# One fused layer on one core: projection weights in one transfer, the head in token halves, a new order of VectorE's attention steps

## The chip, the core and the metric
The kernel runs on one core of a Trainium2 chip. A core has five instruction streams: TensorE (PE; its weight loads are listed as PEld), VectorE (DVE), ScalarE (ACT), GpSimd (POOL) and SyncE (SP). They work side by side and wait for one another only through semaphores. The metric is the device time of one execution in microseconds (us), lower is better.

## The reference, cut to what matters
Input x is 2 sequences of 512 tokens with 256 channels, fp32. "norm" is a layer norm without weights.

```
x = x + attn(norm(x))                    # attn(y) = softmax(causal q k^T / 16) v @ o_proj + y
                                         #   q, k, v = (norm(y) * gamma + beta) @ qkv
x = x + ffn(norm(x))                     # ffn(y) = fp8w(down)((silu(y @ fp8w(gate) * s) * (y @ fp8w(up) * s))) * s
x = x + conv(norm(x))                    # conv(y) = y convolved along 512 steps with a kernel made of
                                         #   exp(dt * A), A from a_real_log, a_imag; C from c_re, c_im; + D * y
x = x + ffn(norm(x))
```

fp8w is a rounding of the weights to the fp8 grid. The convolution's time axis is the one of length 2, so only two taps of its kernel matter.

## The kernel before, in words
Tokens lie in 8 tiles of 128 rows, tiles 0 to 3 for the first sequence, 4 to 7 for the second. Every engine has its program written out by hand; the order of the calls in it is the order of the work, and there is no planner.

**Loads.** SP issues them in this order (lines 231 to 256): tiles 0-1 of x, the q part of `qkv`, tiles 2-3, the k part, four small parameter rows, the v part, tiles 4-7, `o_proj`, scale rows, the gate, up and down weights (768 KB each) and the down scales. ACT issues three small ones (L523 to L527). POOL issues c_re and c_im in `constants` (L287).

**Head.** PE first runs transposes of the identity (`warm_up`, L1065; 14, and 8 more between the q and the k part). `turn_w` (L1073) transposes one part of the projection weights, `fold` (L1080) multiplies q's by k's (`wqk`) and v's by `o_proj` (`wvo`). Tiles are normalised (statistics on DVE, L710 and L713; the inverse deviation by `inverse_std` on POOL, L296 to L306; the scaling by DVE L718 or ACT L539), transposed (`turn_z`, L1088), copied with gamma and beta to `xn_cols` (ACT L510, DVE L729), and multiplied by `wqk` (`make_g`, L1097) and `wvo` (`make_v`, L1104). Each product is copied out of PSUM in two pieces, one by ACT and one by DVE (`g_part`/`g_chunk`, `v_part`/`v_half`).

**Attention loop.** For tile k PE makes `scores` (L1139, with the causal mask L1141), DVE takes the row maxima (`row_max`, L868), ACT the exponentials (`exp_scores`, L577), PE transposes them (`turn_probs`, L1152), ACT copies them (`copy_probs`, L585), PE multiplies by v (`attend`, L1164), DVE finishes the tile (`attention_out`, L873, L876 and its statistics), POOL gives `inverse_std(1, ...)`, ACT normalises (`h_rows`, L569), PE transposes (`turn_h`, L1186), ACT copies the result (`copy_h`, L590) and DVE makes the remainder (`h_tails`, L863).

**Beside it.** DVE computes the parameters of the convolution (`exp_reduce`, `exp_finish`, `exp_times_dt`, `reduce_angle`), the fp8 grids of the three weight matrices (`grid_begin`, `grid_end`, L790 and L795) and lifts and lowers the down weights onto theirs in two halves (`lift_down`, L803; `lower_down`, L809, the last of which is the signal `down_rounded` 2). POOL rounds gate and up (`round_weight`, L413 and L416), makes `x_plus_scales` (L400 to L404), and then in one sequence: `inverse_std(1, 0, 2)`, `taps_begin`, a power (L441), `inverse_std(1, 2, 2)`, a wait for `fit_ready` (DVE's `fit_powers`) and for `down_rounded` 2, six multiplications `down16` (L446), `inverse_std(1, 4, 2)`, `taps_middle`, `inverse_std(1, 6, 2)`, `taps_end` (last line L384) and the first `tail` of the ffn (L456).

**FFN passes.** Four passes of four tiles (two ffn layers). A pass multiplies by gate and up (L1224, 24 blocks of 128 columns in six steps m) and by down (L1258, three steps behind). In pass 0, `spread_taps` (L1269) stands on PE behind step m = 4 of gate and up and waits for the taps; the `down` behind it needs POOL's first tail, which stands behind `taps_end` in POOL's program:

```
if n == 0 and m == 4:
    spread_taps()          # waits for taps_ready
if m >= LAG:
    down(n, m - LAG)       # m - LAG = 1 here: POOL's tail
```

The first gate product with `h_head` waits for both `copy_h`, its product with `h_tail` for both `h_tails`.

Of the kernel before, what the change touches and what calls it, by code (L numbers as in the profile page):

```python
# [34 lines left out]
WARM_UP = 14  # L35
WARM_BETWEEN = 8
# [9 lines left out]
def hybrid_layer(nc, x, qkv, o_proj, gamma, beta, d_param, log_dt, a_real_log, a_imag, c_re, c_im,  # L46
# [13 lines left out]
    with ctx:  # L60
# [48 lines left out]
        param_rows = sb("param_rows", [4 * C, P])  # L109
        params = sb("params", [P, 4 * C])  # L110
        gammas, betas, log_dts, d_params = (params[:, C * n:C * n + C] for n in range(4))
# [33 lines left out]
        q_loaded, k_loaded, v_loaded, wo_loaded = sem("q_loaded"), sem("k_loaded"), sem("v_loaded"), sem("wo_loaded")  # L145
# [19 lines left out]
        w_turned_pe, w_turned_ready = sem("w_turned_pe"), sem("w_turned_ready")  # L165
# [29 lines left out]
        BANK_WT, BANK_WQK, BANK_WVO, BANK_PARAMS, BANK_SCALES, BANK_NORMS = [4, 5, 3], 2, 3, 7, 4, 5  # L195
        BANK_Z = [[0, 1], [4, 5]]
        BANK_G = [[6, 7], [0, 1]]
# [31 lines left out]
        def _(sp):  # L229
# [14 lines left out]
            load_chunks(qkv_sb[:, :, 0:KEY], qkv[:, 0:KEY], q_loaded)  # L244
            load_x(1)
            load_chunks(qkv_sb[:, :, KEY:2 * KEY], qkv[:, KEY:2 * KEY], k_loaded)
            load_rows(param_rows, (gamma, beta, log_dt, d_param), params_loaded)
            load_chunks(qkv_sb[:, :, 2 * KEY:], qkv[:, 2 * KEY:], v_loaded)
            load_x(2)
            load_x(3)  # L250
            load_chunks(wo_sb[:], o_proj, wo_loaded)
# [3 lines left out]
            load_chunks(down_raw[:], down_w, w_loaded[2])  # L255
            sp.dma_start(down_scale_all[:], down_scale.partition_broadcast(P)).then_inc(down_scale_loaded, 16)
# [16 lines left out]
        def _(pool):  # L273
# [11 lines left out]

            def load_s4d(n, array, loaded):
                pool.dma_start(s4d_in[:, n, :].rearrange("p (c n) -> p c n", c=C),  # L287
                               array.rearrange("(c p) n -> p c n", p=P)).then_inc(loaded, 16)
# [97 lines left out]
            def constants():  # L386

                load_s4d(2, c_re, c_loaded)
                load_s4d(3, c_im, c_loaded)
# [43 lines left out]
            inverse_std(0, T, T, twice=True, negative_mean=True)  # L433
            round_weight(0, gate16, gate_up_ready)
            x_plus_scales()
# [3 lines left out]
            taps_begin()  # L439
            pool.wait_ge(bound_squared, 1)  # L440
            pool.tensor_tensor(bound[:, 4, :], bound[:, 3, :], pos_half[:], ALU.pow).then_inc(bound_ready, 1)  # L441
            inverse_std(1, 2, 2, negative_mean=True)
# [58 lines left out]
        def _(act):  # L501
            def turned(w):
                act.wait_ge(w_turned_pe, w + 1)
                act.activation(w_turned[:, w, :, :].rearrange("p c n -> p (c n)"), psum[:, BANK_WT[w], :],
                               ACT.Copy).then_inc(w_turned_ready, 1)

            def xn_chunk(b):
                act.wait_ge(params_ready, 1)
                act.wait_ge(z_turned, C * b + 1)
                act.activation(xn_cols[:, b, 0, :], psum[:, BANK_Z[b][0], :], ACT.Identity, scale=gammas[:, 0:1],  # L510
                               bias=betas[:, 0:1]).then_inc(xn_by_act, 1)

            def g_part(b):
                act.wait_ge(g_made, C * b + 1)
                act.activation(g_cols[:, b, 0, :], psum[:, BANK_G[b][0], :], ACT.Copy,
                               scale=float(KEY) ** -0.5).then_inc(g_by_act, 1)
# [5 lines left out]

            act.dma_start(e_in[:, 0:HN].rearrange("p (c n) -> p c n", c=C),  # L523
# [6 lines left out]
            turned(1)  # L530
            act.wait_ge(tanh_in, 1)
            act.activation(s4d[:, 3, :], s4d[:, 2, :], ACT.Tanh, scale=0.5).then_inc(tanh_out, 1)
            act.wait_ge(wqk_made, 1)
            act.activation(wqk[:].rearrange("p c n -> p (c n)"), psum[:, BANK_WQK, :], ACT.Copy).then_inc(wqk_ready, 1)
            xn_chunk(0)
            turned(2)
# [4 lines left out]
            act.wait_ge(wvo_made, 1)  # L541
            act.activation(wvo[:].rearrange("p c n -> p (c n)"), psum[:, BANK_WVO, :], ACT.Copy).then_inc(wvo_ready, 1)
            g_part(0)
            xn_chunk(1)
# [5 lines left out]
            v_part(0)  # L550
            act.wait_ge(scales_turned, 1)
            act.activation(scales[:], psum[:, BANK_SCALES, 0:2 * M], ACT.Copy).then_inc(scales_ready, 1)
# [40 lines left out]
            square_weights(0)  # L593
            exp_scores(0)
            g_part(1)
            square_weights(1)
            exp_scores(1)
# [4 lines left out]
            for k in range(2, K):  # L602
                exp_scores(k)
                copy_probs(k - 1)
# [87 lines left out]
        def _(dve):  # L692
# [33 lines left out]
            def xn_chunk(b):  # L726
                dve.wait_ge(params_ready, 1)
                dve.wait_ge(z_turned, C * b + 2)
                dve.tensor_scalar(xn_cols[:, b, 1, :], psum[:, BANK_Z[b][1], :], gammas[:, 1:2], betas[:, 1:2],  # L729
                                  ALU.mult, ALU.add).then_inc(xn_by_dve, 1)  # L730

            def g_chunk(b):
                dve.wait_ge(g_made, C * b + 2)
                dve.tensor_scalar(g_cols[:, b, 1, :], psum[:, BANK_G[b][1], :], float(KEY) ** -0.5, None,
# [147 lines left out]
            normalise((0, 1))  # L882
            first_stats(2)
            exp_reduce()
            normalise((2, 3))
            dve.wait_ge(params_turned, 1)
            dve.tensor_copy(params[:], psum[:, BANK_PARAMS, 0:4 * C]).then_inc(params_ready, 1)
# [22 lines left out]
            for k in range(2, K):  # L910
# [4 lines left out]
                if k == K - 1:  # L915
                    fit_powers()
# [417 lines left out]
```

## Time and profile before

| | |
|---|---|
| median of 3 runs | 127.04 us (126.94 to 127.36) |
| the profiled execution | 126.93 us |
| its span in the trace | 125.1 us |
| projection weights' first transposes on PE | 4.79 us |
| first gate product of pass 0 | 51.95 us |
| `spread_taps` | 61.51 us |

The span runs from the first to the last instruction of the core; the 1.8 us by which the execution's time is longer lie around it. All times of rows are counted from the span's start.

### The profile page before, as it was taken

The page shows a single profiled execution, that of the slowest core. Times are in us where ns is not written, and L with a number is a line of the kernel's source. Part 1 is how long each engine was busy: PE and PEld are TensorE (multiplying, and loading weights), DVE is VectorE, ACT ScalarE, POOL GpSimd, SP SyncE. Part 2 cuts the span into 40 slices and gives each one's busy share as a digit, 9 for nine tenths or more (in the row PEclk, how much of TensorE's full clock was granted, in tenths as well). Part 3 has the DMA queues.
Part 4 walks back from the last instruction along what each step waited for, and adds up shares of the span by engine and source line. Part 5 has one row for each costly group of instructions (what it writes and reads, how often), then busy time and mean ns, then how long its engine had stood idle before and what let it go on. Part 6 is the DMA issues. An engine that isn't in the chain of part 4 may idle for free. (4 is left out here: it accounts for less than half of the span.)

```text
span 125.1 us, 2125 instructions
## 1 busy us (share of the span) xinstructions
PE 116.7 (93%) x682; PEld 77.8 (62%) x682; DVE 96.8 (77%) x228; ACT 77.6 (62%) x147; POOL 85.1 (68%) x166
## 2 busy tenths in 40 slices
PE   5996999999999999999999999979999899999970
PEld 5874458668568768645769545567445479755540
DVE  0499999919765876949798889998889965783792
ACT  2325089694874469858865279873587773659800
POOL 2246569999999889888433779697985780037931
PEclk9999999999999999999999999999999999999999
DMA  3999920000000000000000000000000000000404
GB/s 86 305 330 340 339 80 8 0 0 0 0 0 0 5 0 5 0 0 0 0 0 5 0 0 0 0 3 5 0 0 0 3 0 5 0 0 0 168 0 168
DMA packets 5682, 5.80 MB, mean 46 GB/s; under 512 B 1140, under 2 KB 5160, under 8 KB 5672
## 3 DMA queue, kind: packets, MB, share of 16 engines
q1 hardware_dynamic: 4648, 5.52, 13.3%
q10 hardware_dynamic: 960, 0.15, 0.7%
q8 instruction: 5, 0.08, 0.3%
q0 software_dynamic: 64, 0.02, 0.1%
q14 instruction: 5, 0.04, 0.1%
HBM read 4.63 MB, written 1.05 MB: 45 GB/s over the span
## 5 line engine op out<-in xcount | busy, mean ns | idle before, releaser
L618 ACT ACTIVATE gated<-psum,scales 128x512 f32<-128x512 f32 x24 | 16.3, 680 | 12.4 <-PE psum L1224 10.1
L1258 PE MATMUL psum<-down,f_head 128*128 128x256 bf16 x96 | 22.2, 273 | 0.6 <-POOL f_tail L456 0.5
L1258 PE MATMUL psum<-down,f_tail 128*128 128x256 bf16 x96 | 22.1, 272 | 0.0
L456 POOL TENSOR_TENSOR f_tail<-fused,f_head 128x512 f16<-128x512 f32 x11 | 13.0, 1181 | 12.4 <-ACT f_head L624 10.7
L981 DVE SCALAR_TENSOR_TENSOR fused<-psum,up_scales_fit,gated 128x512 f32<-128x512 f32 (+1 forms) x25 | 17.7, 715 | 2.6 <-PE psum L1224 1.3
L624 ACT ACTIVATE f_head<-fused 128x512 f16<-128x512 f32 (+1 forms) x25 | 15.1, 607 | 2.0 <-DVE fused L981 1.7
L989 DVE TENSOR_TENSOR f_tail<-fused,f_head 128x512 f16<-128x512 f32 (+1 forms) x14 | 10.3, 741 | 5.8 <-ACT f_head L624 5.8
L1224 PE MATMUL psum<-h_head,up 128*128 128x512 f16 x44 | 13.1, 379 | 0.1
L1224 PE MATMUL psum<-h_tail,gate 128*128 128x512 f16 x44 | 13.1, 379 | 0.0
L1224 PE MATMUL psum<-h_head,gate 128*128 128x512 f16 x44 | 13.1, 379 | 0.0
L1224 PE MATMUL psum<-h_tail,up 128*128 128x512 f16 x44 | 13.1, 379 | 0.0
L301 POOL TENSOR_TENSOR rstd<-var_eps,neg_half 128x2 f32<-128x2 f32 (+1 forms) x15 | 11.2, 744 | 2.2
L1258 PEld LDWEIGHTS psum<-down,f_head 128*128 128x128 f16 x96 | 9.4, 98 | 4.6 <-POOL f_tail L456 2.1
L1164 PE MATMUL psum<-v_rows,probs_cols 128*128 128x256 f32 x40 | 10.3, 389 | 0.2 <-ACT probs_cols L585 0.2
L1258 PEld LDWEIGHTS psum<-down,f_tail 128*128 128x128 f16 x96 | 9.4, 98 | 1.7
L1139 PE MATMUL psum<-xn_cols,g_cols 128*128 128x128 f32 (+3 forms) x32 | 10.0, 436 | 0.0
L296 POOL TENSOR_SCALAR var_eps<-mean_var 128x2 f32<-128x2 f32 (+1 forms) x15 | 3.8, 256 | 8.7 <-DVE mean_var L713 7.8
L1164 PEld LDWEIGHTS psum<-v_rows,probs_cols 128*128 128x128 f32 x40 | 7.0, 190 | 2.3 <-ACT probs_cols L585 0.8
L1097 PE MATMUL psum<-xn_cols,wqk 128*128 128x512 f32 x16 | 7.4, 603 | 1.0 <-DVE xn_cols L729 1.0
L462 POOL TENSOR_TENSOR x<-scaled_down,x 128x256 f32<-128x256 f32 x8 | 5.6, 725 | 3.6 <-DVE scaled_down L933 3.6
L1224 PEld LDWEIGHTS psum<-h_head,up 128*128 128x128 f16 x44 | 4.2, 98 | 5.5 <-DVE fused L981 0.6
L1224 PEld LDWEIGHTS psum<-h_tail,gate 128*128 128x128 f16 x44 | 4.2, 98 | 5.3 <-DVE h_tail L863 0.4
(176 smaller groups left out, 266.0 us busy)
## 6 DMA issues: line engine op xcount, KB each, us to landing
x_in<-in_x SPq DMA_DIRECT2D x4, 256.0 KB, 4.2
qkv_sb<-in_qkv SPq DMA_DIRECT2D x3, 256.0 KB, 4.1
gate_raw<-in_gate_w SPq DMA_DIRECT2D x1, 768.0 KB, 7.1
up_raw<-in_up_w SPq DMA_DIRECT2D x1, 768.0 KB, 8.9
down_raw<-in_down_w SPq DMA_DIRECT2D x1, 768.0 KB, 10.6
out<-x_in SPq DMA_DIRECT2D x3, 256.0 KB, 2.1
wo_sb<-in_o_proj SPq DMA_DIRECT2D x1, 256.0 KB, 4.7
down_scale_all<-in_down_scale SPq DMA_DIRECT2D x1, 128.0 KB, 10.4
```

Source lines behind the costliest of these rows:

```text
L301: power = pool.tensor_tensor(rstd[:, n, k:k + count], var_eps[:, n, k:k + count], neg_half[:, 0:count], ALU.pow)
L456: pool.tensor_tensor(f_tail[:, m, :], fused[:, m % FUSED, :], f_head[:, m, :], ALU.subtract).then_inc(f_tail_by_pool, 1)
L462: pool.tensor_tensor(new[:, k, :], scaled_down[:, k, :], old[:, k, :], ALU.add).then_inc(ready, 1)
L618: act.activation(gated[:, m % 2, :], psum[:, BANK_GATE[m % 2], :], ACT.Silu, scale=gate_scales[:, m:m + 1]).then_inc(gated_ready, 1)
L624: act.activation(f_head[:, m, cols], fused[:, m % FUSED, cols], ACT.Copy).then_inc(f_head_ready, 1)
L981: dve.scalar_tensor_tensor(out=fused[:, m % FUSED, cols], in0=psum[:, BANK_UP[m % 2], cols], scalar=up_scales_fit[:, m:m + 1], in1=gated[: ...
L989: dve.tensor_tensor(f_tail[:, m, cols], fused[:, m % FUSED, cols], f_head[:, m, cols], ALU.subtract).then_inc(f_tail_by_dve, 1)
L1097: last = pe.matmul(column(BANK_G[b][j], 0, S), wqk[:, c, j * P:j * P + P], xn_cols[:, b, c, :], start=(c == 0), stop=(c == C - 1))
L1139: pe.matmul(column(BANK_S[k % 2], 0, W), g_cols[:, b, j, i * P:i * P + P], xn_cols[:, b, j, 0:W], start=(j == 0), stop=(j == C - 1))
L1164: last = pe.matmul(column(BANK_O[k % 2], 0, H), probs_cols[:, k % 2, t * P:t * P + P], v_rows[:, b, t, :], start=(t == 0), stop=(t == i))
L1224: last = pe.matmul(column(banks[m % 2], 0, S), w[:, c, m * P:m * P + P], part[:, c, :], start=(part is h_head and c == 0), stop=(part is h ...
L1258: last = pe.matmul(down_columns(n, t), part[:, m, t * P:t * P + P], down16[:, m, :], start=(m == 0 and (t % 2 == 0 or n == 2 * B - 1) and ...
```

## The change
The q, k and v parts come in one transfer behind tiles 0-1 of x, with tiles 2-3, `o_proj` and tiles 4-7 behind it. Gamma, beta and d_param rows are loaded by ACT ahead of its own three, the log_dt row is gone (it was not used), and c_re and c_im are loaded by SP behind the down weights. There are 17 warm-up transposes and none later. The first sequence's transposes, `xn_cols` and g are made in halves of two tiles, its v in two pieces, and tiles 0 and 1 are scored before the second half's g. k's turned weights are copied by DVE. DVE, ACT and POOL have new orders; PE has the `attend` of tile 6 ahead of the `turn_probs` of tile 7.

```diff
-WARM_UP = 14
-WARM_BETWEEN = 8
+WARM_UP = 17
...
-        BANK_WT, BANK_WQK, BANK_WVO, BANK_PARAMS, BANK_SCALES, BANK_NORMS = [4, 5, 3], 2, 3, 7, 4, 5
+        BANK_WT, BANK_WQK, BANK_WVO, BANK_PARAMS, BANK_SCALES, BANK_NORMS = [4, 5, 3], 2, 4, 7, 4, 5
-        BANK_G = [[6, 7], [0, 1]]
+        BANK_G = [[5, 2], [0, 1]]
...
             load_x(0)
-            load_chunks(qkv_sb[:, :, 0:KEY], qkv[:, 0:KEY], q_loaded)
+            load_chunks(qkv_sb[:], qkv, qkv_loaded)
             load_x(1)
-            load_chunks(qkv_sb[:, :, KEY:2 * KEY], qkv[:, KEY:2 * KEY], k_loaded)
-            load_rows(param_rows, (gamma, beta, log_dt, d_param), params_loaded)
-            load_chunks(qkv_sb[:, :, 2 * KEY:], qkv[:, 2 * KEY:], v_loaded)
+            load_chunks(wo_sb[:], o_proj, wo_loaded)
             load_x(2)
             load_x(3)
-            load_chunks(wo_sb[:], o_proj, wo_loaded)
...
             load_chunks(down_raw[:], down_w, w_loaded[2])
+            for n, array in ((2, c_re), (3, c_im)):
+                load_chunks(s4d_in[:, n, :].rearrange("p (c n) -> p c n", c=C), array, c_loaded)
...
@@ POOL
             inverse_std(0, T, T, twice=True, negative_mean=True)
+            x_plus_scales()
             round_weight(0, gate16, gate_up_ready)
-            x_plus_scales()
             angle_squares()
             round_weight(1, up16, gate_up_ready)
             inverse_std(1, 0, 2, negative_mean=True)
             taps_begin()
+            inverse_std(1, 2, 2, negative_mean=True)
             pool.wait_ge(bound_squared, 1)
             pool.tensor_tensor(bound[:, 4, :], bound[:, 3, :], pos_half[:], ALU.pow).then_inc(bound_ready, 1)
-            inverse_std(1, 2, 2, negative_mean=True)
             pool.wait_ge(fit_ready, 1)
             pool.wait_ge(down_rounded, 2)
...
@@ ACT
+            load_row(0, gamma)
+            load_row(1, beta)
+            load_row(2, d_param)
...
             turned(0)
-            turned(1)
+            turned(2)
+            xn_half(0)
+            (wqk, then wvo)
+            g_first_half()
             (tanh)
-            (wqk); xn_chunk(0); turned(2)
+            xn_half(1)
             (normed, tiles 4 to 7)
-            (wvo); g_part(0); xn_chunk(1)
+            v_part(0)
             (trig)
-            v_part(0); (scales)
+            xn_second()
             square_weights(0)
+            copy_scales()
             exp_scores(0)
-            g_part(1)
+            exp_scores(1)
+            g_part()
             square_weights(1)
-            exp_scores(1)
             copy_probs(0)
...
             for k in range(2, K):
-                exp_scores(k)
-                copy_probs(k - 1)
+                if k in (3, 6, 7):
+                    copy_probs(k - 1)
+                    exp_scores(k)
+                else:
+                    exp_scores(k)
+                    copy_probs(k - 1)
...
@@ DVE, the whole new order
             first_stats(0); normalise((0, 1)); copy_k(); copy_params(); xn_half(0)
             first_stats(2); first_stats(T); normalise((2, 3)); first_stats(T + 2)
             exp_reduce(); xn_half(1); exp_finish(); exp_times_dt(); reduce_angle()
             grid_begin(0); grid_end(0); row_max(0); row_max(1); g_second_half(); xn_second()
             grid_begin(1); v_half(0); grid_end(1); grid_begin(2); grid_end(2); g_chunk()
             row_max(2); attention_out(0); v_half(1); row_max(3); attention_out(1)
             row_max(4); lift_down(0); attention_out(2); magnitude()
             row_max(5); lift_down(1); attention_out(3); row_max(6); read_norms(); bound_gate_up()
             attention_out(4); row_max(7); lower_down(0); attention_out(5); fit_powers()
             h_tails(0, 0); lower_down(1); h_tails(0, 1); attention_out(6); attention_out(7)
...
@@ PE
-            turn_w(0, q_loaded)
-            warm_up(WARM_BETWEEN)
-            turn_w(1, k_loaded)
+            turn_w(0)
+            turn_w(1)
+            turn_w(2)
...
+            turn_z_half(0)
+            fold(wqk); fold(wvo)
+            make_g_half(0)
+            turn_z_half(1)
+            make_v(0, (0, 1))
...
+            scores(0)
+            scores(1)
+            pe.wait_ge(v_by_act, 1)
+            make_g_half(1)
+            turn_z()
+            make_v(0, (2, 3))
...
             make_g()
-            scores(1)
             turn_probs(0)
             make_v(1)
...
             turn_h(0, 0, first=True)
+            attend(K - 2)
             turn_probs(K - 1)
-            attend(K - 2)
             turn_h(0, 1, first=True)
             attend(K - 1)
```

Lines in brackets and the DVE and PE blocks stand for calls that the full diff writes out. `make_g_half(1)` waits for `v_by_act` because its PSUM bank (2) holds ACT's piece of v.

## Rows read from the trace of the kernel before

**Rows 1.** The page's first part: busy time of each engine over the span.
```profile
PE 116.7 (93%) x682; PEld 77.8 (62%) x682; DVE 96.8 (77%) x228; ACT 77.6 (62%) x147; POOL 85.1 (68%) x166
```

**Rows 2.** A windows table: each engine's busy time in one stretch of pass 0.
```profile
51.95:61.50 9.55, 9.55 (x49) 4.71 (x48) 7.10 (x12) 7.09 (x14) 7.72 (x29) 1.00 0.00 0
```

**Rows 3.** Timeline of PE in the head: start, duration, what, [idle before, releaser].
```profile
1.52 3.25 PE L1065 MATMUL psum<-ident 128*128 128x128 f32 x14 [1.52 <-POOL ident L282]
...
5.48 1.04 PE L1065 MATMUL psum<-ident 128*128 128x128 f32 x8
6.50 0.66 PE L1073 MATMUL psum<-ident,qkv_sb 128*128 128x128 f32 x4
...
10.13 0.60 PE L1073 MATMUL psum<-ident,qkv_sb 128*128 128x128 f32 x4
11.69 3.67 PE L1097 MATMUL psum<-xn_cols,wqk 128*128 128x512 f32 x8 [0.96 <-DVE xn_cols L729]
...
16.92 1.80 PE L1088 MATMUL psum<-ident,normed 128*128 128x128 f32 x8
18.77 3.72 PE L1104 MATMUL psum<-wvo,xn_cols 128*128 128x256 f32 x16
```

**Rows 4.** Timeline of PE in the attention loop and pass 0.
```profile
37.07 1.56 PE L1164 MATMUL psum<-v_rows,probs_cols 128*128 128x256 f32 x6 [0.23 <-ACT probs_cols L585]
...
50.22 1.89 PE L1164 MATMUL psum<-v_rows,probs_cols 128*128 128x256 f32 x8
51.95 0.59 PE L1224 MATMUL psum<-h_head,gate 128*128 128x512 f16 x2
...
61.51 1.05 PE L1269 MATMUL psum<-ident,taps 128*128 128x128 f32 x8
```

**Rows 5.** Timeline of POOL, from the head to pass 0.
```profile
13.50 0.21 POOL L296 TENSOR_SCALAR var_eps<-mean_var 128x4 f32<-128x4 f32 x1 [1.93 <-DVE mean_var L713]
...
17.14 5.16 POOL L413 TENSOR_TENSOR x<-gate_raw,grid 128x512 f32<-128x512 f32 x3 [1.01 <-DVE grid L795]
...
32.53 3.73 POOL L413 TENSOR_TENSOR scaled_down<-up_raw,grid 128x512 f32<-128x512 f32 x3
...
48.29 2.76 POOL L446 TENSOR_SCALAR down<-down_raw,bound 128x256 bf16<-128x256 f32 x6
...
56.05 0.73 POOL L298 TENSOR_SCALAR mean_rstd<-mean_var 128x2 f32<-128x2 f32 x1
...
59.69 0.19 POOL L384 TENSOR_SCALAR taps<-s4d 128x2 f32<-128x2 f32 x1
59.84 1.16 POOL L456 TENSOR_TENSOR f_tail<-fused,f_head 128x512 f16<-128x512 f32 x1
```

**Rows 6.** The page's last part: DMA issues, KB each, us to landing.
```profile
gate_raw<-in_gate_w SPq DMA_DIRECT2D x1, 768.0 KB, 7.1
up_raw<-in_up_w SPq DMA_DIRECT2D x1, 768.0 KB, 8.9
```

**Rows 7.** Timeline of DVE.
```profile
3.69 0.75 DVE L710 BATCH_NORM_STATS2 stats<-x_in 128x6 f32<-128x256 f32 x2 [3.69 <-DMA x_in<-in_x]
...
6.64 0.74 DVE L710 BATCH_NORM_STATS2 stats<-x_in 128x6 f32<-128x256 f32 x2
...
39.80 1.08 DVE L809 TENSOR_TENSOR down_raw<-down_raw,grid 128x768 f32<-128x768 f32 x1
...
51.12 1.25 DVE L863 TENSOR_TENSOR h_tail<-psum,h_head 128x512 f16<-128x512 f32 x2
```

**Rows 8.** Timeline of ACT.
```profile
16.16 2.08 ACT L539 ACTIVATE normed<-x_in,neg_mean_rstd,rstd 128x256 f32<-128x256 f32 x4 [4.53 <-POOL neg_mean_rstd L306]
...
47.84 0.48 ACT L585 ACTIVATE probs_cols<-psum 128x384 f32<-128x384 f32 x1
...
49.34 0.57 ACT L585 ACTIVATE probs_cols<-psum 128x512 f32<-128x512 f32 x1
49.82 1.20 ACT L590 ACTIVATE h_head<-psum 128x512 f16<-128x512 f32 x2
```

## The prediction on record

> **What bounds the kernel now.** I read the page's busy shares, then windows by stage, then the engines' timelines side by side. TensorE is busy for 93% of the span [rows 1], so the question is only where it stands still. In pass 0 it never does: 9.55 of 9.55 us [rows 2]. The chain of waits covers only the last microseconds, which the change does not touch, so it is no help. The reader should see three things in the timelines. First, PE starts its projection work when the weights land and then stops in few places before 51.95, the first gate product: between 10.13 and 11.69, and in the transposes of the second sequence, 16.92 to 18.77, which follow ACT one by one [rows 3]. Second, the loop itself hardly stops [rows 4]. Third, POOL has almost no time to spare: `down16` from 48.29 to `taps_end` at 59.69 + 0.19 = 59.88 is one unbroken sequence of 11.6 us [rows 5], and PE wants its result at 61.51 [rows 4]. That is a reserve of 1.6 us. The passes behind it are PE's work in series, so what 62.4 (the `down` behind `spread_taps`) loses or gains, the end does too.
>
> **Arrival of the weights.** 1.05 MB (two tile pairs with q and k before; one tile pair with q, k and v after) stand at the front of the queue in both kernels. Before, the k part let PE go at 6.50 [rows 3]. x's first pair is there at 3.69 [rows 7]. Lower bound for the whole transfer: 768 KB at the pace of gate and up, whose landings (6.75 + 7.1 and 7.18 + 8.9, issues 0.43 apart) are 2.2 us apart [rows 6], so 5.9. Upper: q needed 1.1 us behind x, three times that is 7.0. I take 6.46, the row with the same bytes. The other moved loads are covered: ACT's three extra issues stand ahead of a table load while ACT has nothing to do, the convolution's small inputs are wanted 5 us later than they land, and c_re and c_im are wanted at 42; on SP they pass only the down scales, which DVE asks for after the attention. POOL's issue time for them (8.75 to 10.4) is saved where POOL then waits for DVE's statistics anyway.
>
> **PE's ledger up to the first gate product.** Before, from 6.50 to 51.95: 45.45 us. Stops in it that belong to the old order: 10.13 to 11.69 is 1.56 for four transposes of 0.11, so 1.1; 16.92 to 18.77 is 1.85 for eight, so 1.0; the `attend` at 37.07 came 0.4 late; smaller ones and the slow first matmul after each stop add 0.7. Together 3.2. Work of the same extent is 42.25. New in it is q's `turn_w` of 0.5, which used to be done ahead. The eight later warm-up transposes ran ahead of 6.50, so dropping them gains nothing. All else on PE is the same work cut differently: 42.75.
>
> New stops, each from durations of rows:
> - `make_g_half(1)` waits for `v_part(0)`. DVE's chain: `copy_k` when two parts are turned (7.8) and 0.7 long, parameters 0.15, the half 0.5, statistics of three pairs at 1.0 each (6.64 and on [rows 7]), the scaling 0.75 in between: 13.2. POOL's `inverse_std` of four tiles takes from 13.50 to ACT's start at 16.16 [rows 5, 8], 2.7; ACT's four tiles 2.08 - 0.1, `v_part` 0.6: 18.5. PE is there at 6.46 + 12 transposes 1.4 + 0.15 + transposes 0.45 + folds 3.45 + half g 1.75 + half z 0.45 + v 1.75 + scores 1.5 = 17.4. Stop 1.2 with the restart.
> - `attend(2)` still comes late behind its copy: 0.4, as before.
> - `attend(6)` needs `copy_probs(6)` right after `turn_probs(6)`: latency 0.3 and 0.48 [rows 8], with only `turn_h` (0.44) beside it: 0.45 with restart.
> - `attend(7)` needs `copy_probs(7)` likewise: 0.3 + 0.57 [rows 8] against 0.44: 0.55. Before, `attend(6)` (1.3) covered this copy; that cover is gone.
>
> Sum 2.6. First gate product: 6.46 + 42.75 + 2.6 = 51.8; call it 51.9, that is no gain worth the name. The new DVE and POOL orders in front of it are hidden: the gate grid comes at 19.6 instead of 17.1, but `x_plus_scales` (4 us) now runs ahead of the rounding instead of behind it, and POOL reaches `inverse_std(1, 0, 2)` some 1 us sooner.
>
> **What comes late next: `lower_down(1)`.** It moves behind `h_tails(0, 0)`, which waits for ACT's `copy_h(0, 0)`, behind `copy_probs(7)`. Let G be the first gate product. `attend(7)` starts as `copy_probs(7)` ends and takes 1.8, so the copy ends at G - 1.9. Then `copy_h` 0.5, `h_tails` 0.65 [rows 7, 8], `lower_down` 1.08 [rows 7]: with overlaps G + 0.25. Two things wait for that:
> - On PE the second gate product needs `h_tails(0, 1)`, now at G + 0.9 instead of G + 0.45: stop 0.55.
> - On POOL all of `down16` to `taps_end` (11.6 us [rows 5]) cannot start before G + 0.35; POOL has been idle since its power, some 5 us. Before, it started at G - 3.7. Taps at G + 11.95, then the tail of 1.16 [rows 5], so `down(0, 1)` at G + 13.15 = 65.05.
> Before it stood at 61.51 + 8 x 0.11 = 62.4. The delay is 2.65 us (the 0.55 lies inside it). ACT's late rows for tiles 6 and 7 stand beside PE's wait and cost nothing more. Nothing behind gives it back, since the later passes hang on PE's own output. Profiled execution: 126.93 + 2.65 = 129.6 us; the median of the runs shown is 0.1 above that execution, which is inside the rounding.
>
> **A rule weighed.** POOL's line at 56.05 took 0.73 where a like one at 59.69 took 0.19, and its rounding took 5.16 beside DVE's grids and 3.73 without them [rows 5]. The Trainium skill ("GPSIMD Engine Reference", Specifications) says that GpSimd shares its SBUF interfaces with VectorE and contends with instructions in a 2-port mode or with two SBUF inputs. The trace agrees. The POOL stretch now runs later, beside more of pass 0's DVE tails. I keep 11.6; without the one 0.5 it would be 11.0, and with two more 12.7, which bounds it.
>
> **Rivals.**
> 1. *PE runs free (the other side).* One mechanism: PE's head is bound by its work alone and none of the four copies makes it wait, the transfer lands at 5.9. Then G = 5.9 + 42.75 = 48.65, and as the late `lower_down` moves with G, `down(0, 1)` is at 61.8: 126.4 us. It decides from G below 49.25 on. For it: the work sum is a row's. Against: the two copies late in the loop are two serial steps with 0.44 beside them.
> 2. *POOL's wait is hidden anyway.* Its reserve of 1.6 us and a sooner `copy_h` swallow the late start, and only PE's short stop at the second gate product is left: 126.93 - 0.05 + 0.55 = 127.4. Against it: the delay of 4 us is more than twice the reserve.
> 3. *TensorE's slow clock.* PE's transposes start every 0.21 us from 1.52 on (14 in 3.25) and every 0.11 from 5.3 on (8 in 1.04 at 5.48) [rows 3]: the lower level, 1.2 GHz, for 3.7 us of activity, then 2.4. The 17 transposes end at 5.15, and nothing follows until 6.46, where there used to be eight more. If the clock does not rise in that gap, transposes and the first fold run at half pace for up to another 3.7 us: 1.85 at most, I take 1.3, since the clock may rise midway: 130.9. The Trainium skill ("TensorE: Matmul & The Clock Gate", "The HAM clock gate") says that the slow level is the default, that activity releases it and idleness brings it back; by that rule this rival's first condition holds, and the trace agrees as far as the rise at 5.3 goes. Against it: this trace stays at the upper level over all PE's later stops, the longest near 1 us.
>
> **How the numbers follow.** Forecast 0.70, at 129.6, its own range 128.4 to 130.5 (arrival 5.9 to 7.0, POOL's stretch 11.0 to 12.7 us, not all at one end). Rival 1: 0.08, a quarter of it within the bound. Rival 2: 0.10, a fifth of it within. Rival 3: 0.12. About 0.3%, 0.4 us, is what runs of this kernel can tell from no change. Faster 0.06, same 0.04, slower 0.90. The range, 128.0 to 131.1, leaves out rivals 1 and 2, 0.18.
>
> **What would show it.** PE's first weight transpose near 6.5 at 0.11 us each; L-lines of `make_g_half(1)` after about 1 us of idleness near 18.5; the first gate product near 51.9, its second part with DVE's `h_tail` as releaser; a POOL idle time of about 5 us ahead of `down16`, released by DVE's `lower_down`; `down16` starting near 52.2; and PE waiting about 2 us for POOL at `spread_taps`, near 63.8. It is wrong if `down16` starts before 50.5, if the first gate product lies before 50, or if `spread_taps` follows the gate and up products without a wait.

## The result, and the profile after

The changed kernel takes 129.12 us in the median of 5 runs (128.27 to 130.91), the kernel before 127.04; the ratio is 1.0122, 95% interval 1.0089 to 1.0154. Slower, as forecast (129.6; 128.0 to 131.1). The ratio, like those below, compares runs without the executions set apart as slow, here the two above 130.5 us, and so is not the quotient of the medians. The profiled execution is the one of 130.91 us, one of these two; where its trace shows a delay that others lack, the text says so. Its span is 129.1 us.

The page: busy time of each engine and the weights' landing (us from issue).

```profile
PE 118.1 (91%) x685; PEld 79.8 (62%) x685; DVE 98.4 (76%) x230; ACT 77.7 (60%) x147; POOL 84.2 (65%) x164
...
qkv_sb<-in_qkv SPq DMA_DIRECT2D x1, 768.0 KB, 4.6
gate_raw<-in_gate_w SPq DMA_DIRECT2D x1, 768.0 KB, 9.1
```

All busy times are within 2 us of [rows 1], and PE's 1.4 us more are less than the slow products seen below add. The loss is in waits. PE's timeline answers to [rows 3, 4]; columns are start, duration, instruction, and idle time with its releaser.

```profile
1.51 3.89 PE L1107 MATMUL psum<-ident 128*128 128x128 f32 x17 [1.51 <-POOL ident L280]
5.86 1.98 PE L1115 MATMUL psum<-ident,qkv_sb 128*128 128x128 f32 x12 [0.46 <-DMA qkv_sb<-in_qkv]
...
17.19 0.22 PE L1206 MATMUL psum<-mask,ident 128*128 128x128 bf16 x1
18.33 1.99 PE L1152 MATMUL psum<-xn_cols,wqk 128*128 128x256 f32 x8 [0.92 <-ACT v_rows L526]
...
49.77 1.99 PE L1229 MATMUL psum<-v_rows,probs_cols 128*128 128x256 f32 x8 [0.25 <-ACT probs_cols L596]
51.60 0.59 PE L1290 MATMUL psum<-h_head,gate 128*128 128x512 f16 x2
...
52.45 0.61 PE L1290 MATMUL psum<-h_tail,gate 128*128 128x512 f16 x2 [0.26 <-DVE h_tail L898]
...
63.58 1.16 PE L1335 MATMUL psum<-ident,taps 128*128 128x128 f32 x8 [1.88 <-POOL taps L378]
64.70 0.28 PE L1324 MATMUL psum<-down,f_head 128*128 128x256 bf16 x1
```

The first gate product has barely moved (51.60 against 51.95), but `spread_taps` is at 63.58 instead of 61.51, behind 1.88 us of idleness where [rows 4] has none. Why POOL is late is read from DVE and POOL.

```profile
50.24 0.69 DVE L898 TENSOR_TENSOR h_tail<-psum,h_head 128x512 f16<-128x512 f32 x1 [1.16 <-ACT h_head L601]
50.84 0.95 DVE L844 TENSOR_TENSOR down_raw<-down_raw,grid 128x768 f32<-128x768 f32 x1
51.71 0.68 DVE L898 TENSOR_TENSOR h_tail<-psum,h_head 128x512 f16<-128x512 f32 x1
```

```profile
51.97 2.76 POOL L438 TENSOR_SCALAR down<-down_raw,bound 128x256 bf16<-128x256 f32 x6 [3.73 <-DVE down_raw L844]
...
63.33 0.19 POOL L378 TENSOR_SCALAR taps<-s4d 128x2 f32<-128x2 f32 x1
63.48 2.27 POOL L448 TENSOR_TENSOR f_tail<-fused,f_head 128x512 f16<-128x512 f32 x2
```

`lower_down(1)` (50.84) stands behind `h_tails(0, 0)`, for which DVE waited 1.16 us; POOL stood idle 3.73 us for it. From `down16` to the last line of the taps it then needs 63.52 - 51.97 = 11.55 us; [rows 5] have 11.59. In this execution something follows that the other traces lack: behind the wait PE's granted clock falls. The windows table of that stretch, columns as in [rows 2]:

```profile
64.70:68.50 3.80, 3.80 (x15) 1.98 (x15) 1.38 (x1) 0.88 (x2) 1.06 (x1) 0.55 0.02 4
```

A mean granted clock of 0.55 is the lower level, 1.2 GHz, for most of 3.8 us, after PE had stood still for 1.88 and then run for 1.1 us at the upper one. It costs some 1.7 us: the kernel before needs 125.1 - 62.4 = 62.7 us from `down(0, 1)` to the end, this execution 129.1 - 64.70 = 64.4. Without it it would have taken 129.2.

### The profile page after: what moved, and what is told of

It is laid out like the page before. It is cut to its first block and busy times, and to the rows that moved or that the text cites. A ratio compares the mean times of both kernels' runs of the same rounds, so it can differ in the third digit from the quotient of the medians.

```text
span 129.1 us, 2131 instructions
## 1 busy us (share of the span) xinstructions
PE 118.1 (91%) x685; PEld 79.8 (62%) x685; DVE 98.4 (76%) x230; ACT 77.7 (60%) x147; POOL 84.2 (65%) x164
## 3 DMA queue, kind: packets, MB, share of 16 engines
HBM read 4.63 MB, written 1.05 MB: 44 GB/s over the span
## 5 line engine op out<-in xcount | busy, mean ns | idle before, releaser
L1324 PE MATMUL psum<-down,f_head 128*128 128x256 bf16 x96 | 22.8, 278 | 0.6 <-POOL f_tail L448 0.5
L1324 PE MATMUL psum<-down,f_tail 128*128 128x256 bf16 x96 | 22.8, 278 | 0.0
L448 POOL TENSOR_TENSOR f_tail<-fused,f_head 128x512 f16<-128x512 f32 x11 | 12.9, 1182 | 12.7 <-ACT f_head L640 11.0
L1031 DVE TENSOR_TENSOR f_tail<-fused,f_head 128x512 f16<-128x512 f32 (+1 forms) x14 | 9.8, 709 | 5.3 <-ACT f_head L640 5.2
L1290 PE MATMUL psum<-h_tail,gate 128*128 128x512 f16 x44 | 13.6, 391 | 0.3 <-DVE h_tail L898 0.3
L1290 PE MATMUL psum<-h_head,up 128*128 128x512 f16 x44 | 13.2, 383 | 0.1
L295 POOL TENSOR_TENSOR rstd<-var_eps,neg_half 128x2 f32<-128x2 f32 (+1 forms) x15 | 11.8, 789 | 2.2
L290 POOL TENSOR_SCALAR var_eps<-mean_var 128x2 f32<-128x2 f32 (+1 forms) x15 | 3.3, 219 | 10.6 <-DVE mean_var L729 9.6
L898 DVE TENSOR_TENSOR h_tail<-psum,h_head 128x512 f16<-128x512 f32 x8 | 5.5, 688 | 3.7 <-ACT h_head L601 3.6
## 6 DMA issues: line engine op xcount, KB each, us to landing
down_scale_all<-in_down_scale SPq DMA_DIRECT2D x1, 128.0 KB, 6.6
```

The costliest lines, as they stand in the source:

```text
L295: power = pool.tensor_tensor(rstd[:, n, k:k + count], var_eps[:, n, k:k + count], neg_half[:, 0:count], ALU.pow)
L448: pool.tensor_tensor(f_tail[:, m, :], fused[:, m % FUSED, :], f_head[:, m, :], ALU.subtract).then_inc(f_tail_by_pool, 1)
L898: dve.tensor_tensor(h_tail[:, :, HALVES[half]], psum[:, BANK_H[half], :].rearrange("p (c s) -> p c s", c=C), h_head[:, :, HALVES[half]], A ...
L1031: dve.tensor_tensor(f_tail[:, m, cols], fused[:, m % FUSED, cols], f_head[:, m, cols], ALU.subtract).then_inc(f_tail_by_dve, 1)
L1290: last = pe.matmul(column(banks[m % 2], 0, S), w[:, c, m * P:m * P + P], part[:, c, :], start=(part is h_head and c == 0), stop=(part is h ...
L1324: last = pe.matmul(down_columns(n, t), part[:, m, t * P:t * P + P], down16[:, m, :], start=(m == 0 and (t % 2 == 0 or n == 2 * B - 1) and ...
```

## The experiments

The baseline, run beside them all, had medians of 126.93 to 127.10 us. Ratios are to it.

**The change once more.** No edit; a second profile.

> The changed kernel itself, once more, for its trace and its spread. Own theory (GpSimd's late start at the down weights costs 2.3 us up to the first down product behind the taps): that wait is there in every trace, about 2.0 us at spread_taps, whether the execution is one near 128.3 or one near 130.9 us; what differs between executions is TensorE's pace right behind the wait (0.11 or 0.21 us between down products), worth up to 1.9 us. Rival (the pace of TensorE is the main loss): an execution near 128.3 would show little or no wait at spread_taps. Time: 128.3 to 131, most near 129.

128.96 us (128.3 to 130.39, 6 runs), ratio 1.0167, interval 1.0131 to 1.0204. In its profile (130.39 us) the clock stays up behind the taps, 11.98 us behind the first gate product again, but in the head PE is slow for longer:

```profile
6.05 2.82 PE L1115 MATMUL psum<-ident,qkv_sb 128*128 128x128 f32 x12 [0.65 <-DMA qkv_sb<-in_qkv]
...
9.90 1.89 PE L1122 MATMUL psum<-w_turned 128*128 128x256 f32 x8
```

Twelve transposes take 1.53 us at full pace; here 2.82, in the first profile 1.98. The four transposes of x behind them are slow here too, so the first fold (9.90) comes 3.85 us behind the first weight transpose. So the gate product is at 52.74. What is the same in both is the distance from the gate product to the taps.

**One line back.** The changed kernel with `lower_down(1)` ahead of `h_tails(0, 0)`:

```diff
+lower_down(1)
 h_tails(0, 0)
-lower_down(1)
 h_tails(0, 1)
```

> The changed kernel with lower_down(1) in front of h_tails(0, 0), where VectorE stands idle for 1.16 us, and nothing else. Own theory: down16 starts at 50.05 instead of 51.97, the wait at spread_taps shrinks from 2.0 to about 0.4 us, the second gate product's wait of 0.42 us is gone, and with so short a wait TensorE's pace does not fall: 127.3 us, between 127.0 and 127.6, with a spread like that of the kernel before. Rival 1 (the loss lies in TensorE's own order at the end of the attention loop or in the head, not in GpSimd's start): 128.3 or more stays. Rival 2 (the slow pace is brought on by the pause in the head, not by the wait at the taps): executions near 130.5 still occur.

127.07 us (126.62 to 130.78, 12 runs), ratio 0.9998, interval 0.9983 to 1.0013: the whole loss is gone. PE and POOL:

```profile
50.78 0.59 PE L1290 MATMUL psum<-h_head,gate 128*128 128x512 f16 x2
...
61.23 1.16 PE L1335 MATMUL psum<-ident,taps 128*128 128x128 f32 x8 [0.78 <-POOL taps L378]
62.34 0.28 PE L1324 MATMUL psum<-down,f_head 128*128 128x256 bf16 x1
```

```profile
49.33 2.76 POOL L438 TENSOR_SCALAR down<-down_raw,bound 128x256 bf16<-128x256 f32 x6 [1.89 <-DVE down_raw L844]
```

But this isn't the kernel before again: the gate product comes 1.17 us earlier than there, and PE gives 1.11 of it back at the taps, which are 10.45 us behind the gate product instead of 9.56, with 1.11 instead of 0.89 for the spread. `lower_down(1)` is still late for POOL, by 1.89 us.

**The late call alone.** The kernel before, with only this edit:

```diff
 if k == 4:
-    lower_down(1)
     magnitude()
 ...
 h_tails(0, 0)
+lower_down(1)
 h_tails(0, 1)
```

> The kernel before with one part of the change alone: lower_down(1) between h_tails(0, 0) and h_tails(0, 1). Own theory: in this kernel h_tails(0, 0) is later still (51.1), so lower_down ends near 52.7, down16 starts 4.5 us later than before (52.8), the taps are ready at 64.4, and the down product behind them comes 3.2 us late: 130.2 us, and up to 132.1 in executions in which TensorE's pace halves behind the wait. Rival (GpSimd's chain has room, the loss comes from the new order of the loop): under 128.

130.17 us (129.77 to 130.61, 4 runs), ratio 1.0245, interval 1.0229 to 1.0261. One call moved in an otherwise old kernel makes more than the whole loss. PE and POOL:

```profile
52.69 0.59 PE L1224 MATMUL psum<-h_head,gate 128*128 128x512 f16 x2
54.04 0.60 PE L1224 MATMUL psum<-h_tail,gate 128*128 128x512 f16 x2 [0.76 <-DVE h_tail L863]
...
64.96 1.16 PE L1269 MATMUL psum<-ident,taps 128*128 128x128 f32 x8 [1.67 <-POOL taps L384]
```

```profile
53.56 2.75 POOL L446 TENSOR_SCALAR down<-down_raw,bound 128x256 bf16<-128x256 f32 x6 [5.16 <-DVE down_raw L809]
```

The taps are 12.27 behind the gate product, and `down(0, 1)` 13.39 instead of 10.46: 2.93 us. The other 0.74 us by which this execution (130.61 us) is longer than the one before (126.93) lie ahead of the gate product, in a head that the edit does not touch: eight warm-up transposes took 1.85 us instead of 1.04. Between the medians of this kernel and the changed one lies 1.05 us: what the rest of the change is worth.

**PE kept busy in the wait.** The changed kernel with 16 identity transposes into a free PSUM bank ahead of `spread_taps`:

```diff
 if n == 0 and m == 4:
+    for _ in range(16):
+        pe.transpose(column(BANK_H[1], 0, P), ident[:], ident[:])
     spread_taps()
```

> The changed kernel with 16 transposes of the identity into a PSUM bank not in use, in front of spread_taps in pass 0: work of 1.75 us inside TensorE's wait of 2.0 us, nothing on the path. Own theory (two costs: 2.3 us of late taps, and in some executions half pace behind the wait, 1.9 us): the first stays, the second goes: 128.3 to 128.8 us with no execution near 130.6. Rival (half pace is set off in the head): executions near 130.6 still occur and the median stays at 129.

129.01 us (128.28 to 130.64, 5 runs), ratio 1.0134, interval 1.0115 to 1.0153. The taps stay 11.94 us behind the gate product (62.61 and 50.67), so PE's idleness is not their cause; two of five executions are still near 130.6 although PE no longer stands still there, so the idleness in front of the taps is not what sets those two apart. Whether it brings on the fall of the clock seen in the first profile is not shown: the record lists a mean granted clock for each execution, 0.987 for that one and 0.996 or more for the ten others of the changed kernel and the five of this one.

The profiled execution (128.28 us) also shows what the changed kernel takes when nothing is slow. PE in its head:

```profile
5.71 1.53 PE L1115 MATMUL psum<-ident,qkv_sb 128*128 128x128 f32 x12 [0.61 <-DMA qkv_sb<-in_qkv]
...
7.82 1.89 PE L1122 MATMUL psum<-w_turned 128*128 128x256 f32 x8
```

Against the second profile of the change (130.39 us) it is 2.11 us shorter, and 2.07 of these lie ahead of the gate product: weights 0.34 earlier, and 2.11 instead of 3.85 us from the first weight transpose to the first fold. So that long execution is one with a slow head, and not one with a longer wait for the taps.

**Longer warm-up.** The one-line kernel, with `WARM_UP = 21`.

> The kernel with lower_down(1) in front of h_tails(0, 0) (127.07 us, executions 126.62 to 130.78), and 21 warm-up transposes in place of 17, which fills the 0.4 to 0.6 us between the last warm-up transpose and the weights' landing at 5.8. Theory A (the pause delays the rise of TensorE's clock): the pace is up when the weights land, in every execution; the executions near 130 are gone, median 126.7 to 127.0. Theory B (the moment of the rise differs from execution to execution by itself, as it did in the kernel before with a late lower_down, whose pause was 0.24 us and whose pace rose only near 7.6): the spread stays, median 127.0 to 127.3, and where the rise is late PE's first weight transpose is also up to 0.1 later than the landing, since 21 slow transposes end at 5.95.

127.36 us (126.71 to 127.72, 12 runs), ratio 1.0004, interval 0.9977 to 1.0031. In its profile (127.54 us) the pause is gone and the rise is late all the same:

```profile
6.04 2.09 PE L1115 MATMUL psum<-ident,qkv_sb 128*128 128x128 f32 x12
```

The pause is thus not needed for a late rise. No execution is above 127.72 this time; with two such (129.09, 130.78) among 12 of the other kernel, that shows little.

**v's copy two tiles earlier.** The one-line kernel, with ACT's `v_part(0)` in the middle of its four tiles:

```diff
 for k in range(T, K):
     ... # normed[:, k, :]
+    if k == T + 1:
+        v_part(0)
-v_part(0)
```

> The kernel with lower_down(1) in front of h_tails(0, 0) (127.07 us), and ACT's v_part(0) after two of its four normalised tiles instead of after all four. Theory A (make_g_half(1) stops for v_part(0), as forecast at 1.2 and seen at 0.75 + 0.10 in that kernel's profile at 16.7): the stop goes, v_part runs from about 15.9, PE's first gate product comes 0.8 earlier near 49.95; but POOL's down16 waits for lower_down(1), which comes earlier only as far as DVE's row maxima do. If the whole stretch moves, 126.2 to 126.4. Theory B (the head's next wait takes its place: the four tiles of the second sequence end 0.55 later on ACT, or DVE's and POOL's work on x is the bound): turn_z or the first score waits instead, the first gate product stays near 50.7 and the time at 127.0.

126.07 us (125.81 to 129.29, 9 runs), ratio 0.992, interval 0.9887 to 0.9953. `make_g_half(1)` follows the mask without a stop:

```profile
16.52 0.22 PE L1207 MATMUL psum<-mask,ident 128*128 128x128 bf16 x1
16.58 1.95 PE L1153 MATMUL psum<-xn_cols,wqk 128*128 128x256 f32 x8
```

The gate product moves from 50.78 to 49.80 (0.84 by the stop and its slow first product, the rest by weights that landed earlier), `down16` from 49.33 to 48.31 and the taps from 61.23 to 60.16: the whole stretch moves, and the stop was worth its whole length.

**PE's order at the end of the loop.** The one-line kernel with each copy of the probabilities under a product (the loop's last calls written out, `scores` left out):

```diff
-attend(5); turn_probs(6); turn_h(0, 0); attend(6); turn_probs(7); turn_h(0, 1); attend(7)
+turn_probs(6); attend(5); turn_h(0, 0); turn_probs(7); attend(6); turn_h(0, 1); attend(7)
```

> The kernel with lower_down(1) in front of h_tails(0, 0) (127.07 us), and PE's order at the end of attention changed: turn_probs(6) ahead of attend(5), turn_probs(7) ahead of attend(6), so that each copy of the probabilities has a product beside it. Theory A (the two stops forecast at 0.45 and 0.55, and seen at 0.41 and 0.52 with their slow first product, belong to this order): both go, the first gate product is near 50.0; taps still hang on lower_down(1), whose DVE queue is full, so PE's wait for the taps grows from 0.94 to about 1.6 and the total gains only 0 to 0.3: 126.8 to 127.1. Theory B (the stretch is bound elsewhere, by ACT or by the rows of the second half): turn_h(0, 1) or attend(7) waits instead, the first gate product stays at 50.6 or later.

127.17 us (126.84 to 129.32, 12 runs), ratio 1.0004, interval 0.998 to 1.0029. Both stops go (gate product at 50.00), and nothing is gained:

```profile
48.27 1.89 PE L1229 MATMUL psum<-v_rows,probs_cols 128*128 128x256 f32 x8
...
61.32 0.93 PE L1339 MATMUL psum<-ident,taps 128*128 128x128 f32 x6 [1.65 <-POOL taps L378]
```

The taps are where they were (61.23), and so is the start of `down16` (49.25 against 49.33). Here POOL's chain is the bound, and a PE that comes earlier waits longer.

**The c loads back on POOL.** The one-line kernel, with POOL issuing c_re and c_im in `constants`.

> The kernel with lower_down(1) in front of h_tails(0, 0) (127.07 us), with the loads of c_re and c_im issued by POOL in constants() again, as in the kernel before. Theory A (moving them to SP is worth nothing either way, as forecast: POOL waits for DVE's statistics there, SP's line behind the scales has nothing anyone waits for): within 0.2 of 127.07, although SP's two issues took 3.72 and 1.80 us. Theory B (POOL's issue time of some 1.7 us sits in front of inverse_std(0, 4, 4), on which ACT's normalised tiles and so v_part(0) and make_g_half(1) wait): the stop at make_g_half(1), 0.75 in that kernel, grows by up to 1 us, 127.5 to 128.1.

127.91 us (127.51 to 128.47, 10 runs), ratio 1.0049, interval 1.0028 to 1.0070, against 0.9998: theory B. POOL, then PE:

```profile
10.61 0.95 POOL L381 DMA_DIRECT2D s4d_in<-in_c_re  x1
11.57 0.73 POOL L381 DMA_DIRECT2D s4d_in<-in_c_im  x1
...
13.51 0.20 POOL L288 TENSOR_SCALAR var_eps<-mean_var 128x4 f32<-128x4 f32 x1
```

```profile
18.23 1.13 PE L1153 MATMUL psum<-xn_cols,wqk 128*128 128x256 f32 x4 [1.48 <-ACT v_rows L527]
```

`inverse_std(0, 4, 4)` starts at 13.51 instead of 12.83, where it had waited 0.89 for DVE; ACT's tiles, `v_part(0)` and `make_g_half(1)` follow.

**The spread one step later.** The changed kernel with `spread_taps` behind `down(0, 1)`.

> The changed kernel itself (129.12 and 128.96 us), and spread_taps behind down(0, 1) instead of in front of it. Theory A (in the changed kernel PE's 2 us at spread_taps are the whole loss, and nothing but PE's order makes them: the taps are not wanted for 0.9 us more): down(0, 1), 8 products of 0.11 = 0.88 us, runs inside the wait, spread_taps still starts 11.98 behind the first gate product, and the time falls by 0.8 to 0.9, to 128.1 to 128.3. Theory B (POOL's lateness reaches further than spread_taps: its tails f_tail behind taps_end, or down16's own last parts, are late for PE as well): PE waits again at down(0, 1) or behind it, and the time falls by less than 0.4.

131.1 us (129.14 to 131.53, 6 runs), ratio 1.0297, interval 1.0252 to 1.0342. Both theories had it wrong; it is slower. PE, then POOL, of its fastest execution:

```profile
63.73 0.28 PE L1324 MATMUL psum<-down,f_head 128*128 128x256 bf16 x1 [2.95 <-POOL f_tail L448]
...
64.61 1.06 PE L1335 MATMUL psum<-ident,taps 128*128 128x128 f32 x8
```

```profile
62.37 0.19 POOL L378 TENSOR_SCALAR taps<-s4d 128x2 f32<-128x2 f32 x1
62.52 2.27 POOL L448 TENSOR_TENSOR f_tail<-fused,f_head 128x512 f16<-128x512 f32 x2
```

`down(0, 1)` needs POOL's first tail, 1.16 us long and behind the taps. The spread used to run beside this tail; now its 0.9 us come behind it. That explains 1 us (the next gate product is 14.82 behind the first, and 13.99 in the second profile of the change). Why five of the six executions were slower still, by 0.7 to 2.4 us, their lack of a trace leaves open. The record lists a mean granted clock of 0.986 or 0.987 for four of them, as for the first profile of the change, where a fall of the clock cost 1.7 us, and 0.999 for the fastest. PE's wait of 2.95 us is the longest in any of these kernels, but one untraced execution each of two kernels with short waits or none there, 129.29 and 128.72 us in the v and the all-waits experiment, has 0.986 and 0.987 too, so that this wait is the cause is not shown.

**All waits together.** The one-line kernel with the two edits of ACT and PE above, and a shorter way to `down16`:

```diff
 # POOL
-inverse_std(1, 2, 2, negative_mean=True)
 ... # the bound's power
+inverse_std(1, 2, 2, negative_mean=True)
 pool.wait_ge(fit_ready, 1)
-pool.wait_ge(down_rounded, 2)
 for m in range(M):
+    if m == 0 or m == M // 2:
+        pool.wait_ge(down_rounded, 1 + m // (M // 2))
 # DVE
 lower_down(0)
+fit_powers()
 attention_out(5)
-fit_powers()
 lower_down(1)
```

> Both of the two edits above, and the way to down16 made short: POOL takes the power for the bound ahead of inverse_std(1, 2, 2), DVE does fit_powers ahead of attention_out(5), and down16 begins with its first half when lower_down(0) is done. Theory A (all that is left between the two kernels is these waits): first gate product near 49.2, down16's first line near 46.5 and its last near 49.5, taps near 58.7, PE waits for them 0.3 at most; 124.9 to 125.5 us, below both kernels. Theory B (POOL's chain after down16 doesn't move, since inverse_std(1, 4, 2) and the taps then run beside DVE's h_tails and tails and get longer): taps near 60 and 125.8 to 126.4.

125.66 us (125.03 to 128.72, 6 runs), ratio 0.9866, interval 0.9821 to 0.9910: faster than both kernels, and between the two theories' ranges. PE:

```profile
48.31 0.66 PE L1253 MATMUL psum<-ident,h_rows 128*128 128x128 f32 x4 [0.76 <-ACT h_rows L582]
...
50.62 0.59 PE L1296 MATMUL psum<-h_head,gate 128*128 128x512 f16 x2
...
60.12 1.05 PE L1341 MATMUL psum<-ident,taps 128*128 128x128 f32 x8
```

Pass 0 has no wait again (9.50 us from the gate product to the spread), but the power, 1.34 us on POOL, now stands ahead of the rows that `turn_h(0, 1)` wants; ACT waited 1.62 us for POOL there.

**Two attempts to have both.** First `inverse_std(1, 2, 2)` ahead of the power again, and `spread_taps` behind step 5 (ACT's copy of the taps behind its gate 5):

> The kernel with all four waits shortened (125.66 us), with inverse_std(1, 2, 2) ahead of the bound's power again, since its profile showed PE waiting 0.92 us at turn_h(0, 1) for the rows which that power delayed, and with spread_taps one place later (behind gate and up product 5, ACT's copy of the taps behind its gate 5). Theory A: the stop at turn_h(0, 1) goes, the first gate product is near 49.6; down16 starts near 48.3 and the taps are there near 60.4, PE comes for them at 61.7 and doesn't wait; 124.6 to 125.0. Theory B (the reserve is used up: ACT's copy of the taps and head(0, 4) are late for copy_h(1, 0) and pass 1): the gain behind pass 0 is lost again at the start of pass 1, 125.3 to 125.8.

127.01 us (126.75 to 128.87, 12 runs), ratio 0.9989, interval 0.9968 to 1.0011. DVE waited 1.37 us for the power with `attention_out(5)` behind it, and `down(0, 1)` for POOL's tail:

```profile
61.37 0.28 PE L1330 MATMUL psum<-down,f_head 128*128 128x256 bf16 x1 [1.12 <-POOL f_tail L449]
```

Then the same with the spread in its old place and `attention_out(5)` ahead of `fit_powers`:

> The kernel with all waits shortened and inverse_std(1, 2, 2) ahead of the bound's power, with the two faults that the profile of the last version (127.01 us) showed taken out: spread_taps stands again in front of down(0, 1), since down(0, 1) itself waits for POOL's first f_tail (1.16 us behind the taps), beside which the spread is free; and DVE does attention_out(5) ahead of fit_powers, since fit_powers waited 1.37 us for the power with attend(7) behind it. Theory A (POOL's sequence from down16 to the first tail sets down(0, 1), and G + 12.0 at the latest): attend(7) starts without a stop near 47.5, first gate product near 49.3, down16 starts near 47.5, taps near 59.3, down(0, 1) near 60.5 against 61.1 in the 125.66 us kernel: 125.0 to 125.3. Theory B (DVE is full from 43 to 49, so lower_down(1) ends no earlier than 49 and holds up h_tails or the second half of down16): down(0, 1) near 61.3 and 125.7 to 126.2.

126.01 us (125.52 to 126.48, 6 runs), ratio 0.9915, interval 0.9886 to 0.9945. No gain over the 125.66; the profiled execution (126.48 us, twelve transposes in 2.35) has the gate product at 50.07 and the taps at 60.85, behind a wait of 1.12 us. So POOL's sequence takes back what PE wins. I read the two orders as two ways to pay for one power, which no run isolates.

## Why the prediction was right, step by step

- *Arrival of the weights, 6.46.* Mis-sized: 5.86 here, 5.65 to 6.05 in the other profiles of the new head. The lower bound was the better value.
- *PE's ledger, 42.75 plus 2.6 of stops.* Good. From 5.86 to 51.60 are 45.74 us; 0.45 are the slow transposes (1.98 - 1.53), and the four stops with their slow first products are 1.18 (forecast 1.2), 0.34 (0.4), 0.41 (0.45) and 0.51 (0.55), 2.44 together. That leaves 42.85. The first stop is so long only here, where DVE waited 0.69 us for x's third pair; in the filled kernel and the one-line kernel it is 0.84. The terms named for it on DVE also add up to 12.9, not to the 13.2 that was used.
- *First gate product 51.9.* 51.60 here, by errors that cancel: weights 0.6 early, but 0.45 of slow transposes and 0.34 of longer stop. Where the transposes run at full pace it is 50.67 to 50.78. So "no gain worth the name" was wrong for those executions: the new head is worth up to 1.3 us. The one-line experiment shows that it is spent again at the taps.
- *`lower_down(1)` at G + 0.25 and `down16` at G + 0.35.* Measured: the call ends at 51.79, G + 0.19, and `down16` starts at G + 0.37. POOL's idle time was 3.73, not 5, because its power starts and ends later than I had it; nothing hung on that.
- *PE's stop at the second gate product, 0.55.* 0.42, and inside the longer delay, as said.
- *Taps at G + 11.95, then the tail.* G + 11.98 here, 11.98 in the second profile and 11.94 in the filled kernel; the tail's 1.16 was the right term for `down(0, 1)`, and I overlooked my own sentence when I planned to move the spread.
- *`down(0, 1)` at 65.05, 2.65 late.* 64.70, 2.3 late, and 129.2 for the sum without the later slow products; the median is 129.12. From the gate product to `down(0, 1)` the forecast is met: 13.10 us here against 13.15. That the total fits as well is in part luck. An execution of this order with a fast head ends at 128.3 (lowest of both series 128.27 and 128.3, traced at 128.28 in the filled kernel), 1.35 above the kernel before and not 2.65, since its gate product comes 1.28 earlier than there. The median lies higher by delays of single executions that the sum did not hold.
- *The c loads.* Costed at nothing on the ground that POOL waits for DVE there. It waited 0.89 us, and the two issues take 1.68. Left on POOL they would have cost 0.8 us (127.91 against 127.07). The forecast of the stop (1.2) had them moved already, so the sum was not hurt.
- *The Trainium skill's rule on GpSimd's shared interfaces ("GPSIMD Engine Reference", Specifications).* POOL's stretch of 11.6 ran beside other DVE work and took 11.55 and 11.56 in the two profiles of the change and 11.34 in the late-call kernel, but 11.79 to 12.02 in the five kernels that differ from the one-line kernel by nothing or one edit, where it starts earlier. So a later start did not lengthen it, as I had feared. The bounds of 11.0 and 12.7 were wider than needed; how much of the 0.7 us between these profiles is the rule's contention, no run here isolates.
- *Rival 3, the slow clock.* Its mechanism as told (the gap between 5.15 and the weights) is not borne out as the cause, since with the gap filled PE's pace rose late too. Its outcome is there, though: PE is slow into the weight transposes in some executions, by 0.45 to 1.7 us, and the traced one with 1.7 took 130.39, near this rival's 130.9. The other traced long one, 130.91, has 0.45 of it and 1.7 of the later fall, which no rival had. I gave it 0.12 as if it were one case for all executions; it is a share of them. Its first step also read a level of the clock off the spacing of transposes: the profile's granted clock is 1.00 in that stretch of every trace here, whatever the spacing.
- *Rivals 1 and 2.* Rival 1 set G below 49.25; it was 51.60. Rival 2's reserve of 1.6 us was really swallowed first: `down16` started 3.7 us later and the taps' step on PE 2.07.

## What to carry to other kernels

When a helper's result feeds a long chain on another engine, place it by that chain's length and not by the moment its own inputs are ready: one 0.95 us call behind a wait cost 2.0 us here and 3.2 in the kernel before (medians; 1.5 and 2.9 from the gate product to `down(0, 1)` in the profiles), because 11.6 us of POOL's work hung on it. Before a stop is removed ahead of such a join, ask whether the other chain starts earlier by it too: the stop in the head moved both engines and was worth its length (126.07), the two at the end of the loop moved PE alone and were worth nothing (127.17). Before a waiting step is moved, ask what else stands behind the same producer: `spread_taps` was free only because it ran beside the tail that `down(0, 1)` waited for.

## What the hardware did that I had not expected

The moment at which PE's pace doubles differs between executions of kernels with the same head, from within the warm-up transposes to about 9.9 us, and moves the end by up to 1.7 us; twelve equal transposes took 1.53, 1.60, 1.98, 2.09, 2.35 or 2.82 us. The profile's granted clock reads 1.00 all the while, so this slow pace is seen only in the spacing of the instructions; in the fall behind the taps the granted clock shows it. The Trainium skill ("TensorE: Matmul & The Clock Gate", "The HAM clock gate") says that the number of slow products at the start differs from run to run; these traces agree. What decides it in one execution stays open. Of the executions that are 2 us or more longer than others of their kernel two were traced: one is explained by its slow head and later weights (2.07 us), the other by 0.93 us ahead of the gate product and the fall of the clock (1.7); the causes of the rest stay open.

Two small transfers took SP long to issue, though SP had nothing else to do. In the first profile of the change, SP's queue:

```profile
5.51 0.72 SPq L233 DMA_DIRECT2D down_raw<-in_down_w  x1
6.27 3.72 SPq L233 DMA_DIRECT2D s4d_in<-in_c_re  x1
10.04 1.80 SPq L233 DMA_DIRECT2D s4d_in<-in_c_im  x1
11.88 0.90 SPq L254 DMA_DIRECT2D down_scale_all<-in_down_scale  x1
```

In the other profiles with them on SP they took 1.66 to 2.85 and 1.91 to 2.57, on POOL 0.95 and 0.73. Nobody waits for them here; in front of a load that is wanted soon, I expect such 3.8 to 5.5 us to be the price, which no run shows.
